# A two-layer attention and expert kernel: merged heads put in another PSUM bank, routing steps moved closer, and the second layer's expert weights loaded once

## The reference, cut to what matters

```python
x = x + _L0_xattn_ref(_layernorm(x), ctx, ctx, encoding, Wq, bq, Wk, bk, Wv, bv, Wm, bm)  # 16 heads of 8, rotary
x = x + _L0_ffn_ref(_layernorm(x), gate_w, w13, w2)          # 64 experts, best 8, inner 128
x = x + _L1_xattn_ref(_layernorm(x), ctx, ctx)               # one 256x256 softmax per batch
x = x + _L1_ffn_ref(_layernorm(x), router_w, expert_bias, gate_proj, up_proj, down_proj)  # 16 experts, best 4, inner 224
```

## Time and profile before

| what | value |
|---|---|
| median of 3 runs | 686.94 us (686.65 to 692.87) |
| the profiled execution | 690.62 us |
| its span in the trace | 688.9 us |
| TensorE's mean granted clock | 0.838 |
| PE, DVE, ACT, POOL busy | 482.5, 384.4, 221.6, 349.4 us |
| moved by DMA | 163.95 MB, mean 238 GB/s |

### The profile page before, as it was taken

How to read it: one execution, slowest core, us unless ns; L and a number is a source line. 1 busy time by engine, 2 the same in 40 slices (tenths; PEclk the granted TensorE clock), 3 DMA queues, 4 the chain that set the end, 5 groups by cost and what they waited for, 6 DMA issues and landing times.

```text
span 688.9 us, 12080 instructions
## 1 busy us (share of the span) xinstructions
PE 482.5 (70%) x3519; PEld 368.4 (53%) x3519; DVE 384.4 (56%) x1235; ACT 221.6 (32%) x578; POOL 349.4 (51%) x476
## 2 busy tenths in 40 slices
PE   0741898888898430699989994157764499999960
PEld 0630344444443210688877783145553499999950
DVE  8981576788786460154444442689955044444426
ACT  0451065555667310333323331134431122222210
POOL 9394221115556673256545537014444867777730
PEclk9985599888899655799999998597765599999985
DMA  5089989746588697789999723961111799999927
GB/s 184 4 203 244 341 291 298 218 94 155 166 238 279 208 402 285 229 270 313 347 298 309 244 95 106 353 273 55 70 69 61 258 388 360 349 353 361 375 100 276
DMA packets 82915, 163.95 MB, mean 238 GB/s; under 512 B 13070, under 2 KB 58142, under 8 KB 81072
## 3 DMA queue, kind: packets, MB, share of 16 engines
q1 hardware_dynamic: 56832, 106.20, 46.3%
q0 software_dynamic: 13968, 32.29, 12.7%
q10 hardware_dynamic: 12064, 24.84, 12.4%
HBM read 104.94 MB, written 66.78 MB: 249 GB/s over the span
## 4 chain that ended last, share of the span: by engine, by line
PE 32%; DMA 13%; DVE 9%; issue 2%; POOL 2%; ACT 1%; SPq 1%; POOLq 0%; DVEq 0%
PE sc_ps L1790 11%; DMA hd_side<-held 6%; PE hd_ps_up L1246 6%; PE sc_ps L1772 5%; DMA rows<-hd_side_out,hd_side_target 3%; PE hd_ps_out L1252 2%; DMA sc_rows<-rows 2%; PE hd_ps_x L1224 2%; PE sc_ps L1780 1%; DVE sc_rows L1879 1%; PE sc_ps L1740 1%; POOL rows L1393 1%; PE sc_ps L1728 1%; DVE sc_n_stats L1473 1%; DMA listed<-sc_empty,sc_index 1%
## 5 line engine op out<-in xcount | busy, mean ns | idle before, releaser
L1021 DVE TENSOR_REDUCE at_top<-at_ps_top 128x2 f32<-128x512 f32 x128 | 83.2, 685 | 46.4 <-PE at_ps_top L926 45.6
L1393 POOL DMA_INDIRECT rows<-hd_out,hd_rows x64 | 62.2, 972 | 59.3 <-DVE hd_out L1344 36.9
L1093 ACT ACTIVATE at_prob<-at_ps_score 128x512 f32<-128x512 f32 x128 | 72.6, 594 | 51.2 <-PE at_ps_score L944 50.6
L926 PE MATMUL at_ps_top<-e_arena 96*128 96x256 bf16 x256 | 57.6, 315 | 37.2 <-PEq L107 21.9
L1246 PE MATMUL hd_ps_up<-hd_x_turned,e_arena 128*128 128x160 f32 x512 | 82.7, 305 | 0.0
L1790 PEld LDWEIGHTS sc_ps<-sc_t_turned,e_w 128*112 128x112 f32 x672 | 80.6, 180 | 2.6
L1790 PE MATMUL sc_ps<-sc_t_turned,e_w 128*112 128x128 f32 x672 | 82.0, 276 | 0.0
L1246 PEld LDWEIGHTS hd_ps_up<-hd_x_turned,e_arena 128*128 128x128 f32 x512 | 76.1, 192 | 8.7 <-issue 6.2
L682 POOL DMA_INDIRECT held<-e_extended,e_address x64 | 62.4, 975 | 28.4 <-issue 17.7
L682 POOL DMA_INDIRECT listed<-e_extended,e_address x32 | 33.6, 1049 | 69.0 <-DVE e_address L674 61.5
L1381 DVE TENSOR_TENSOR hd_inner<-hd_silu,hd_ps_up 128x160 f32<-128x160 f32 x64 | 20.5, 321 | 81.8 <-ACT hd_silu L1331 81.8
(11 more groups left out here) (266 smaller groups left out, 911.6 us busy)
## 6 DMA issues: line engine op xcount, KB each, us to landing
e_w<-in_weights SPq DMA_DIRECT2D x42, 704.0 KB, 6.0
e_arena<-in_weights SPq DMA_DIRECT2D x52, 384.0 KB, 11.4
held<-e_empty ACTq DMA_DIRECT2D x16, 960.0 KB, 7.2
hd_rows<-held SPq DMA_DIRECT2D x15, 768.0 KB, 10.5
sc_rows<-rows SPq DMA_DIRECT2D x8, 1024.0 KB, 13.8
sc_tile_rows<-listed SPq DMA_DIRECT2D x42, 144.0 KB
parts<-op_parts SPq DMA_DIRECT2D x8, 576.0 KB, 6.7
e_arena<-in_weights ACTq DMA_DIRECT2D x12, 384.0 KB, 4.0
```

Of the source, the lines that this page charges most:

```text
L926: last = nc.tensor.matmul(ps_top[at % TOPS][:, half, :], q_in[n][0:TOP, columns(at, half)], k_in[n][0:TOP, columns(at)], start=True, stop= ...
L1021: nc.vector.reduce_max(top[:, 2 * h:2 * h + 2], ps_top[at % TOPS][:], AX_X).then_inc(top_found, 1)
L1093: nc.scalar.activation(prob[at % RING][:], ps_score[at % SCORES][:], ACT.Exp, scale=scale).then_inc(prob_ready, 1)
L1393: nc.gpsimd.indirect_dma_start(rows_out, to, out_ap, None, bounds_check=TOKENS * LAYER0.chosen - 1, oob_is_err=False).then_inc(semaphore, 16)
```

## The change

Three parts are changed.

- **Bank.** The merged heads (`ps_merged`) move from the bank of the routing to the upper half of the bank in which the maxima are turned (`ps_rows`). `merge` waits no longer for the routing of the batch before, but for `keep_rows` and for the residual of the batch before; some `turn_tops` wait for `lift_known` or for `x_ready`.
- **Steps.** The pieces of routing get new offsets, most of them nearer to the batch's end; the last two batches get lists of their own. The scatters of a batch are spread over ten steps so that none lies in the step of `cut_tops`. `turn_tops`, `keep_rows` and `place` are issued one step later.
- **Weights.** All 16 experts' weights of the second layer get their own place in SBUF (`experts.w`, 16 times 704 KB) and are loaded once, three at a time behind the rows of batches 4 to 7 and the last four after them. To make room, `rows` is a ring of five, so the rows of batches 5 to 7 are loaded when a batch's `x_kept` is there. In the tile loop SP loads no weights; ACT reads the expert's number into a register and copies the up weights (128 x 896) to one of two fixed buffers (`copy_up`), and PE reads the number too and takes the down weights at an address made from it.

```diff
-    LOAD, SHARE = 26, 34
-    AMID = dict(load=LOAD, share=SHARE, merge=37, add=38, scale=39, norm=42, turn=46, keep=47, score=51, choose=52, expo=55, rank=55,
-                places=57, targets=59, weights=62, scatter=62)
-    LAST_BUT_TWO = dict(AMID, turn=45, keep=46, score=49, choose=49, expo=50, targets=50, rank=50, places=51, weights=51, scatter=53)
-    LAST_TWO = dict(load=LOAD, share=SHARE, merge=35, add=36, scale=37, norm=37, turn=39, keep=39, score=41, choose=41, expo=42, targets=42,
-                    rank=43, places=43, weights=43, scatter=46)
+    AMID = dict(load=26, share=34, merge=37, add=38, scale=39, norm=42, turn=45, keep=46, score=49, choose=50, expo=52, rank=53,
+                places=54, targets=55, weights=57)
+    LAST_BUT_TWO = dict(AMID, score=48, choose=48, expo=49, rank=49, places=50, targets=50, weights=51)
+    LAST_BUT_ONE = dict(load=26, share=31, merge=32, add=33, scale=34, norm=34, turn=36, keep=36, score=38, choose=38, expo=39, targets=39,
+                        rank=40, places=40, weights=40)
+    LAST = dict(load=26, share=34, merge=35, add=36, scale=37, norm=37, turn=39, keep=39, score=41, choose=41, expo=42, targets=42,
+                rank=43, places=43, weights=43)
+    SCATTERS = (57, 58, 60, 61, 62, 64, 65, 66)
+    LAST_SCATTERS = tuple(range(51, 59))
...
-                hh, late = divmod(at + LEAD - 4, HALF)
+                hh, late = divmod(at + LEAD - 5, HALF)
                 if late == HALF - 1 and 0 <= hh < HALVES:
                     turn_tops(hh)
...
+                if hh == 1:
+                    pe.wait_ge(lift_known, 1)
+                if hh >= 6 and hh % 2 == 0:
+                    pe.wait_ge(x_ready, hh // 2 - 2)
...
             def merge(b):
-                if b >= B - 2:
-                    pe.wait_ge(routing.rank_read, b)
-                elif b >= 1:
-                    pe.wait_ge(routing.logits_read, b)
-                else:
-                    pe.wait_ge(lift_known, 1)
+                pe.wait_ge(rows_kept, min(2 * b + 6, HALVES))
+                if b >= 1:
+                    pe.wait_ge(x_ready, b)
                 pe.wait_ge(divided, b + 1)
...
             for b in range(B):
+                if b >= ROWS_IN:
+                    sp.wait_ge(x_kept, b - ROWS_IN + 1)
                 sp.dma_start(rows[b][:], by_batch[b]).then_inc(rows_loaded[b], 16)
...
+                if b >= ROWS_IN - 1:
+                    for e in range(EARLY * (b - ROWS_IN + 1), EARLY * (b - ROWS_IN + 2)):
+                        experts.load(sp, e)
+            for e in range(EARLY * (B - ROWS_IN + 1), E):
+                experts.load(sp, e)
             last = groups(sp)
             columns = [experts.column(sp, 0, u) for u in range(U)]
-            for u in range(2):
-                experts.load(sp, columns[u], u)
             sp.wait_ge(experts.scattered, 16 * layer.chosen * B)
...
                     load_tile(i, u, c)
-                    sp.wait_ge(down_done, i * U + u - U + 1)
-                    sp.sem_inc(sp_parted, 1)
-                    experts.load(sp, c, u)
...
+            def down(i, u):
+                e = experts.expert(pe, i, u)
+                pe.wait_ge(inner_ready, i * U + u + 1)
...
+            def copy_up(i, u):
+                e = experts.expert(act, i, u)
+                nc.scalar.activation(up_w[u % 2][:].rearrange("p k n -> p (k n)"), experts.up(e), ACT.Copy).then_inc(up_copied, 1)
...
                 nc.scalar.activation(silu[u % 2][:], ps_up[u % 2][:, 0, :], ACT.Silu).then_inc(silu_done, 1)
+                if not (final and u >= U - 2):
+                    copy_up(i if u + 2 < U else i + 1, (u + 2) % U)
```

More of the change, by code:

```diff
@@ L406, in __init__ @@
         self.layer = layer
-        U, E = range(layer.unroll), layer.experts
+        E = layer.experts
         self.extended = s.sbuf("extended", [P, B, ROW1], F32)
@@ L415, in __init__, with up, down @@
         down_at = 4 * layer.inter
-        self.w = [s.sbuf(f"w{u}", [P, down_at + layer.chunks * D], F32) for u in U]
-        self.up = [w[:, 0:down_at].rearrange("p (k n) -> p k n", k=2) for w in self.w]
-        self.down = [w[0:layer.width, down_at:].rearrange("p (c n) -> p c n", c=layer.chunks) for w in self.w]
+        self.words, self.down_at = down_at + layer.chunks * D, down_at
+        self.w = s.sbuf("w", [P, E * self.words], F32)
         self.weights_dram = weights_dram
-        self.loaded = [s.sem(f"weights_loaded{u}") for u in U]
+        self.loaded = s.sem("weights_loaded")
         self.scattered = s.sem("scattered")
+    def up(self, e):
+        return self.w[:, bass.ds(e * self.words, self.down_at)]
+    def down(self, e, c):
+        return self.w[0:self.layer.width, bass.ds(e * self.words + (self.down_at + c * D), D)]
     def column(self, engine, i, u):
@@ L768, in __init__ @@
                 self.batch[stage, b * H + offset] = b
+            for k, offset in enumerate(self.SCATTERS if b < B - 3 else self.LAST_SCATTERS):
+                self.scatters.setdefault(b * H + offset, []).append((b, k))
         self.end = max(at for _, at in self.batch) + 1
[L770 to L775, removed]
         self.first_scatter = min(self.scatters)
@@ L873, in _ @@
             for at in range(-LEAD, END):
-                hh, late = divmod(at + LEAD - 5, HALF)
+                hh, late = divmod(at + LEAD - 6, HALF)
                 if late == HALF - 1 and 0 <= hh < HALVES:
@@ L1005, in _ @@
                 if b is not None:
-                    if b + 1 < B - 2:
-                        pe.wait_ge(x_ready, b + 2)
                     routing.pe_rank(pe, b)
@@ L1578, in second_phase @@
     most_groups = layer.tiles // U
-    up_w, down_w, weights_loaded = experts.up, experts.down, experts.loaded
+    ROWS_IN, EARLY = 5, 3
     with ExitStack() as stack:
         s = Space(nc, stack, "sc_", joined)
-        rows = [s.sbuf(f"rows{b}", [P, chosen, D], F32) for b in range(B)]
+        ring = [s.sbuf(f"rows{n}", [P, chosen, D], F32) for n in range(ROWS_IN)]
+        rows = [ring[b % ROWS_IN] for b in range(B)]
+        last_rows = [ring[b // 2][:, b % 2 * layer.chosen:(b % 2 + 1) * layer.chosen, :] for b in range(B)]
         norms = TwoNorms(nc, s)
@@ L1590, in second_phase @@
         vals_shared = [s.sbuf(f"vals_shared{n}", [P, 2, P], F32) for n in range(2)]
+        up_w = [s.sbuf(f"up_w{n}", [P, 2, experts.down_at // 2], F32) for n in range(2)]
         empty = s.sbuf("empty", [P, ROW1], F32)
@@ L1649, in _ @@
                 load_tile(0, u, columns[u])
-            sp.wait_ge(tile_loaded[1], 16)
-            for u in range(2, U):
-                experts.load(sp, columns[u], u)
             with sp.Fori(1, last + 1) as i:
@@ L1789, in up @@
                         for k in range(2):
-                            op = nc.tensor.matmul(ps_up[u % 2][:, part, c * P:(c + 1) * P], up_w[u][:, k, at:at + W],
+                            op = nc.tensor.matmul(ps_up[u % 2][:, part, c * P:(c + 1) * P], up_w[u % 2][:, k, at:at + W],
                                                   t_turned[u % 2][:, k, :], start=k == 0, stop=k == 1)
@@ L1797, in step @@
                 if not (first and u < 2):
-                    down(i * U + u - 2, (u - 2) % U)
+                    down(i if u >= 2 else i - 1, (u - 2) % U)
                 up(i, u)
@@ L1809, in _ @@
                 step(last, u, final=True)
-            down(last * U + U - 2, U - 2)
-            down(last * U + U - 1, U - 1)
+            down(last, U - 2)
+            down(last, U - 1)
         @block.scalar
@@ L1857, in step @@
                 nc.scalar.activation(silu[u % 2][:], ps_up[u % 2][:, 0, :], ACT.Silu).then_inc(silu_done, 1)
+                if not (final and u >= U - 2):
+                    copy_up(i if u + 2 < U else i + 1, (u + 2) % U)
+            act.wait_ge(experts.loaded, 16 * E)
+            for u in range(2):
+                copy_up(0, u)
             keep_turned(0, 0)
```

45 lines of the change are left out of this document (23 added, 22 removed).

## The result

The changed kernel takes 706.35 us (median of 4 runs, 704.40 to 708.82), and the kernel before 686.88 (also 4 runs, 686.65 to 692.87): a ratio of 1.026 (95% interval 1.020 to 1.033). The forecast was 687.6 with a range of 677 to 700, so the time lies outside it. The two traces differ by 17.4 us (spans of 706.3 and 688.9), somewhat less; the traced execution of the kernel before was 3.7 us above its median and that of the kernel after 2.5. This is where the time went. A half batch is eight heads, from the start of its first exponential to that of the next half batch's.

A forecast was written before the change was run, and what follows sets the result against it. Bounds: PE and DVE holding each other up in attention, POOL at the scatters, PE in the tile loop. 690.62 - 3 + 2.5 + 4 - 2.8 = 691.3; the same +0.7 on the median 686.94 gives 687.6 us, range 677 to 700.

The forecast's parts named there:

- DVE's work closer together: +4 us: Attention steps: joined routing pieces on DVE lengthen gaps PE waits in, 1.0 us a batch over four batches.
- a loss comes back only in steps in which PE is the faster of the two: Attention steps: about half the steps win lost time back, so 2.1 us a batch was taken as 1.0.
- the bound for pieces paid in full: Attention steps: +8.4 us if nothing of DVE's 2.1 us a batch is won back in four batches.
- the slower rival: Attention steps: DVE's gaps cost 8.4 us, PE's waits about 21.5 instead of 13.1; 696 us, chance 0.19.
- The clock goes with it: Attention steps: longer PE waits can bring the granted clock's fall to 0.50 in more batches; no size given.
- Rows of maxima, +2.5 (0 to +5): Attention steps: rows issued one step later while score stays; three waits lengthen by 0.84 us each, +2.5 us.
- the 6 named as a sign: Attention steps: PE's waits for the rows of maxima would be near 6 us.
- Scatters' end, -3: End of the routing: batch 4's earlier weights bring POOL's last scatters forward, -3 us, bounds -5 and 0.
- foretold idle time before the sixth batch: POOL's last scatters: the next batch ready only one step earlier, behind the last-but-one's share; about 1 us idle.
- Weights once, -2.8: Tile loop's start: without two weight loads the clear takes 3 us, the tile's load 2.2; -2.8, bounds -4.5 and -1.
- the rival on PE's sequencer: Tile loop: PE's register load not hidden, each of 42 tiles 0.7 us longer, +29, 717 us; chance 0.09.
- The 3.4 us a tile: Tile loop: sequencer at 0.062 us for each of 44 instructions plus 0.7, some 25 us slower; chance 0.03.

The follow-up runs named there:

- old_steps: The kernel after with the offsets and scatter steps of the kernel before; ratio 1.002 to the kernel before.
- filler: The kernel after with 20 and 10 products that nobody reads in PE's two waits of each batch; ratio 1.007 to the kernel before.
- rows_later: The kernel before with only the rows of maxima turned, kept and placed one step later; ratio 1.010, +7.0 us.
- weights_once: The kernel before with only the second layer's part of the change (weights once, ACT's copy, rows in a ring); ratio 0.994, 4.0 us less.
- two_again: weights_once with the first two experts' weights loaded a second time before the tile loop, ACT's first copy waiting for them; ratio 1.006 to the kernel before.
- bank_plain: The kernel before with the second layer's part, merged heads in the new bank and the lift's product in the routing's bank; ratio 0.9925.

## Why the prediction was wrong

**The step that failed is "DVE's work closer together: +4 us",** and in it two sentences. The first: "a loss comes back only in steps in which PE is the faster of the two, and that is about half of them", which halved 2.1 us a batch. In the sum nothing came back. PE's waits for maxima grew by 9.6 us against before (13.1 to 22.7) and by 11.4 against old_steps, where the bound for pieces paid in full was 8.4; the slower rival had foretold 21.5. The second: "The clock goes with it", which got no price. It cost 10 us in half batches 7 to 14 (filler), more than the waits. The earlier trace rows had shown the price: two us at 0.50 with PE full and DVE no longer the bound. In after the clock fell at or within 2.2 us behind three of the four waits of 2.7 us and all four of the 1.47 us that follow `scale`; in before at four of the eight waits of 1.2 us, in old_steps at two. The length of the single wait doesn't decide it alone: the shorter of after's two waits was the surer one. Together the offsets were put at +1 us (+4 on DVE, -3 at the scatters) and measured +17.

**Rows of maxima, +2.5 (0 to +5),** was mis-sized: +7.0 in rows_later, about 5 of it in half batches 1 to 6. The waits grew by 1.9 us there, near the term (in after to 3.8 us, not to the 6 named as a sign). The clock at the first exponentials, at 0.50 in every kernel with the rows late, was not in it; that it is the rest of the 7 us is likely and not shown.

**Scatters' end, -3:** in the trace the last scatter comes 2.6 us sooner against the last exponential, and the held phase's first load 1.6. The first scatter's gain was foretold at 4.2 and is 5.1; foretold idle time before the sixth batch about 1, measured 3.04. The cause named for that idle time, the seventh batch's `share` ahead of the sixth's work, was right; that DVE would stand for that batch's heads to land was missed. Half batches 15 and 16, +3.9 us at clocks of 0.65 and 0.75, had no term and were not isolated.

**Weights once, -2.8,** held: -3.4 in the trace, -4.0 in weights_once. The clear landed in 2.47 us (put at 3) and the tile in 2.17 (2.2), and two_again puts the time back, most of it by the same two landings. ACT's copy took 0.95 us (0.84 to 0.98) and is hidden; PE's register read is hidden with room for a second. From the first up product to the last a tile takes (678.91 - 562.08) / 41 = 2.85 us, and in before (661.28 - 544.47) / 41 = 2.85; the prediction's 2.80 was read from PE's sequencer, which was further ahead of the engine at the last tile than at the first. The period did not change, so the rival on PE's sequencer falls. The 3.4 us a tile that the prediction had estimated from the Trainium skill (TensorE: Matmul & The Clock Gate, section "Wait — 56ns, not 53.3ns?") are not borne out either: no run here shows a sequencer that slow.

The terms as measured, on times: weights -4.0, rows +7, offsets +17; together +20 beside 19.5 for the whole change. Taken singly the offsets' parts were 9 (`choose`), 9 (`places`) and 3 us (the ends), 21 in all; each has an interval of 3 to 6 us, so the difference to 17 says nothing.

## What to carry to other kernels

Where two engines hold each other up through a short ring, count what an in-order engine does between two items of the ring as one gap: pieces put side by side there are waited for in full, while the same pieces one or two items apart were free. Price a longer idle time of PE twice, for itself and for the clock that may fall behind it; here, with PE the bound in the steps that followed, the second cost at least as much as the first. And before a step is made earlier on an in-order engine, look at what it must wait for: all that stands behind it waits too.

## What was not expected of the hardware

The granted clock followed PE's idleness closely enough to be steered: 20 and 10 products that nobody reads, 2.35 and 1.26 us, in PE's waits kept it at 1.00 (2.4 GHz) for 80 us in which it had fallen to 0.50 (1.2 GHz) seven times, and the kernel became 13 us faster with the work added. A fall cost about 1.5 us (10.4 us over seven). Where the waits were 1.2 us, as in bank_plain, the same cure was worth 1.5 us in the trace and nothing that the times can show.
